# Rounding and an epsilon add given to GpSimd, and a different order of the first batch's parts, T4, weights and moved low parts, in a two-layer float32 kernel on one core

## The chip, the cores and the metric

The kernel runs on one core of one Trainium2 chip. The metric is device time in microseconds (us), from the first to the last instruction with what the launch adds around them; a smaller number is better. The engines are TensorE (PE), VectorE (DVE), ScalarE (ACT), GpSimd (POOL) and SyncE (SP), which only issues DMAs; ScalarE issues some DMAs too.

## The reference

There are 16 batches of 512 tokens with 512 features, in float32. Each batch names a language and an expert.

```python
# layer 0, per batch
h = relu(x @ aW1[lang] + ab1[lang])                  # 512 -> 128
u = x + h @ aW2[lang] + ab2[lang]                    # 128 -> 512
normed = (u - mean(u)) * rsqrt(var(u) + 1e-5)
x = x + normed * gamma[lang] + beta[lang]
# layer 1, per batch
h = gelu(x @ W1 + b1)                                # 512 -> 2048
out = x + concat(h @ W2 + b2, h @ We[expert] + be[expert])   # 2048 -> 384 and 128
```

## The kernel before

A float32 product is made of three passes in the type fp32r: every operand is split into a high part (HI, the value rounded) and a low part (LO, the value minus HI), and HI·HI, HI·LO and LO·HI are added up in PSUM (`three_passes`, L255 to L257). So every operand costs a rounding (an ACT copy, mostly) and a subtraction (DVE or POOL).

The batches go in eight pairs. For the second layer a pair is one matrix product by Strassen's scheme with seven products: x1 is cut into B11, B21, B22 and B12, their sums T1 to T4 take the place of some of them, and the weights W1 are kept with their sums S1 to S4. A pair has eight steps (k = 0 to 7, GROUPS = 8). Step k makes 4 x 128 of the hidden features: the products `pe_p1` to `pe_p7` into the banks up_a, up_b, up_c, and from them the tiles C11, C12, C22, C21. DVE adds the partial sums (`dve_sum_q`, `dve_sum_u2`, `dve_sum_c12`, `dve_sum_c22`, `dve_sum_c21`), ACT applies Gelu and rounds (`act_g`, `act_g_hi`), and DVE makes the low part (`dve_g_lo`, L899). `pe_down` then multiplies by W2 into the four `down` banks: C11 and C21 are the two halves (h = 0, 1) for the pair's batch 0, C12 and C22 for batch 1. `dve_down_sum` adds every second step's result to `resid`. Beside this, steps 0 to 7 do the first layer of the next pair (`pe_adapter_up`, `pe_adapter_down`, `dve_add_adapter`, `dve_moments`, `pool_rsqrt`, `dve_finish`).

The first pair is different. Its first layer runs ahead of everything else, and its W1 and W2 are rounded, summed and split while they are used: `pool_weight_sums(k)` makes S1 to S4 once the load has landed, `act_w1_hi(k)` rounds, `dve_w1_lo(k)` subtracts, `keep_w1` stores the result in DRAM for the later pairs, and `pe_p1` needs HI and then LO (`first_p1`, L299 and L307). For k = 1 and k = 8 (which is step 0 of the second pair) the subtraction is shared: `dve_rest_w1_lo` does four of the seven parts and `pool_first_w1_lo` the other three.

The first batch's bias b2 is added by a matmul: one row of b2 is rounded (`act_b2_hi`, L702), `dve_b2_lo` makes its low row (L957), and `pe_first_b2` (L505) multiplies by ones. In the first batch `act_first_part` copies each transposed block out of PSUM twice (L715 the value itself, L716 the rounded one), `pe_first_low` (L535) subtracts the rounded one in PSUM, and `act_first_low` (L720) copies the low part out. `first_hi` and `first_lo` (L276, L277, L282) are the products of step 0, collected by `first_half`.

The order of the work on each engine is written out by hand; each engine runs its list in order and waits on semaphores. An instruction that waits holds back all that stands behind it on its engine, DMA issues on ACT and SP included. `pool_rsqrt` waits for `dve_var`, the variance with epsilon added (L947, L976 on DVE), and takes it to the power of minus one half.

Of the kernel before, what the change touches and what calls it, by code (L numbers as in the profile page):

```python
# [26 lines left out]
def build(nc, xT, x, lang, expert, a_w1, a_b1, a_w2, a_b2, a_gamma, a_beta,  # L27
# [126 lines left out]
    dve_u, dve_st, dve_mv, dve_var, dve_gm, dve_x1 = (  # L154
        sem(n) for n in ("dve_u", "dve_st", "dve_mv", "dve_var", "dve_gm", "dve_x1"))
# [89 lines left out]
    FIRST_B11, FIRST_B21 = (up_a, down[1]), (down[2], down[1])  # L245
# [162 lines left out]
    def pe_down(eng, pr, b, k):  # L408
# [9 lines left out]
        for h in range(2):  # L418
# [19 lines left out]
        if opens:  # L438
# [500 lines left out]
    def dve_moments(eng, m, b, t):  # L939
# [7 lines left out]
        eng.tensor_scalar(var_eps[:, n - 1:n], mean_var[:, b, t, 1:2], EPS, None, ALU.add).then_inc(dve_var, 1)  # L947
# [20 lines left out]
    def dve_first_moments(eng, b, t, bank):  # L968
# [899 lines left out]
```

## Time and profile before

| | before |
|---|---|
| median of 3 runs | 1453.47 us (1453.41 to 1453.83) |
| the profiled execution | 1455.1 us |
| its span | 1453.3 us |
| PE busy | 1442.8 us, 99% |
| DVE busy | 949.9 us, 65% |
| POOL busy | 652.7 us, 45% |
| ACT busy | 524.8 us, 36% |
| granted TensorE clock | 1.0 in the whole span |

The profiled execution is the one that all rows come from. Its time is its span and 1.8 us around it. A row of a timeline gives the start in us from the span's start, the time in us, the engine, the line, the operation, output<-inputs and how many instructions it merges; in brackets stands the idle time of the engine before it, with what ended it.

### The profile page before, as it was taken

How to read it: one execution, taken by the hardware profiler on the slowest of the kernel's cores; microseconds unless marked ns; L12 is line 12 of the kernel's file. 1: busy time of each engine (PE TensorE's matmuls, PEld its weight loads, DVE VectorE, ACT ScalarE, POOL GpSimd, SP SyncE). 2: the span in 40 equal slices, each digit the busy share in tenths (PEclk: the TensorE clock that was granted, in tenths of full speed). 3: DMA queues.
4: the chain of work that ended last, by engine and by line, in shares of the span. 5: the costliest groups of instructions: out<-in, count | busy, mean ns of one | idle time of the engine just before them, and what ended most of it. 6: DMA issues, size and time to landing. Idle time of an engine off the chain costs nothing.

```text
span 1453.3 us, 19122 instructions
## 1 busy us (share of the span) xinstructions
PE 1442.8 (99%) x6444; PEld 1185.0 (82%) x6444; DVE 949.9 (65%) x1596; ACT 524.8 (36%) x854; POOL 652.7 (45%) x640
## 2 busy tenths in 40 slices
PE   9999999999999999999999999999999999999999
PEld 5778888888888888888888888888888888888887
DVE  6899786775567756667557675577656676554444
ACT  4633454232433225232352333433234322432231
POOL 5996466441473514834138341384323743341101
PEclk9999999999999999999999999999999999999999
DMA  7857577553466545564455644646446454364332
GB/s 237 272 165 243 180 245 249 171 195 132 167 224 182 185 148 178 202 212 148 159 192 186 206 151 154 231 146 213 177 137 236 156 191 159 109 218 159 131 109 87
DMA packets 127764, 263.02 MB, mean 181 GB/s; under 512 B 12210, under 2 KB 84402, under 8 KB 119604
## 3 DMA queue, kind: packets, MB, share of 16 engines
q1 hardware_dynamic: 117876, 158.78, 34.3%
q10 hardware_dynamic: 9792, 103.03, 18.3%
q8 instruction: 52, 0.85, 0.2%
q14 instruction: 44, 0.36, 0.1%
HBM read 224.02 MB, written 37.75 MB: 180 GB/s over the span
## 4 chain that ended last, share of the span: by engine, by line
PE 90%; DVE 3%; POOL 3%; issue 2%; ACT 1%; ACTq 0%; DMA 0%; SPq 0%; DVEq 0%; POOLq 0%
PE down L255 15%; PE down L257 15%; PE down L256 15%; PE up_b L255 5%; PE up_b L257 5%; PE up_b L256 5%; PE up_c L257 3%; PE up_c L256 3%; PE up_c L255 3%; PE up_a L255 3%; PE up_a L256 3%; PE up_a L257 3%; DVE g L899 1%; POOL resid L1270 1%; PE aux L518 1%
## 5 line engine op out<-in xcount | busy, mean ns | idle before, releaser
L255 PE MATMUL down<-w,g 128*128 128x512 f32 x1024 | 401.1, 392 | 0.9 <-DVE g L899 0.9
L257 PE MATMUL down<-w,g 128*128 128x512 f32 x1024 | 398.6, 389 | 0.0
L256 PE MATMUL down<-w,g 128*128 128x512 f32 x1024 | 398.5, 389 | 0.0
L1277 POOL TENSOR_TENSOR w<-w_raw,ones 128x256 fp32r<-128x256 f32 x128 | 90.5, 707 | 616.2 <-DMA w_raw<-m_we 616.1
L255 PEld LDWEIGHTS down<-w,g 128*128 128x128 f32 x1024 | 192.3, 188 | 42.4 <-DVE g L899 3.2
L899 DVE TENSOR_TENSOR g<-g_raw,g 128x512 fp32r<-128x512 f32 x256 | 211.4, 842 | 23.1 <-ACT g L671 20.9
L257 PEld LDWEIGHTS down<-w,g 128*128 128x128 f32 x1024 | 192.2, 188 | 40.3
L256 PEld LDWEIGHTS down<-w,g 128*128 128x128 f32 x1024 | 192.3, 188 | 39.0
L663 ACT ACTIVATE g_raw<-up_a,m_b_sb 128x512 f32<-128x512 f32 x64 | 44.1, 690 | 407.7 <-PE up_a L257 383.0
L894 DVE TENSOR_TENSOR g_raw<-up_b,s 128x512 f32<-128x512 f32 x63 | 43.5, 691 | 222.0 <-PE up_b L257 178.3
L671 ACT CAST g<-g_raw 128x512 fp32r<-128x512 f32 x256 | 159.0, 621 | 8.1
L663 ACT ACTIVATE g_raw<-u,m_b_sb 128x512 f32<-128x512 f32 x63 | 45.6, 724 | 252.0 <-PE down L257 230.6
L255 PE MATMUL up_b<-bo,w 128*128 128x512 f32 x336 | 131.6, 392 | 2.2 <-DVE u L879 1.4
L256 PE MATMUL up_b<-bo,w 128*128 128x512 f32 x336 | 130.8, 389 | 0.0
L257 PE MATMUL up_b<-bo,w 128*128 128x512 f32 x336 | 130.8, 389 | 0.0
L918 DVE TENSOR_TENSOR resid<-down,resid 128x512 f32<-128x512 f32 x128 | 86.6, 690 | 57.9 <-PE down L257 57.9
L1279 POOL TENSOR_TENSOR w<-w_raw,w 128x256 fp32r<-128x256 f32 x128 | 106.5, 832 | 10.1
L663 ACT ACTIVATE g_raw<-g_raw,m_b_sb 128x512 f32<-128x512 f32 x63 | 45.5, 722 | 161.0 <-DVE g_raw L894 161.0
L1270 POOL TENSOR_TENSOR resid<-x,m_bias 128x512 f32<-128x512 f32 x64 | 93.0, 1482 | 0.0
L257 PE MATMUL up_c<-bo,w 128*128 128x512 f32 x224 | 87.2, 389 | 0.0
L255 PE MATMUL up_c<-bo,w 128*128 128x512 f32 x224 | 87.2, 389 | 0.0
L256 PE MATMUL up_c<-bo,w 128*128 128x512 f32 x224 | 87.1, 389 | 0.0
(239 smaller groups left out, 2508.3 us busy)
## 6 DMA issues: line engine op xcount, KB each, us to landing
w<-w_kept ACTq DMA_DIRECT2D x55, 1792.0 KB, 7.6
w<-w_kept SPq DMA_DIRECT2D x56, 768.0 KB, 4.9
w_raw<-m_we SPq DMA_DIRECT2D x128, 128.0 KB, 4.6
out<-resid SPq DMA_DIRECT2D x64, 256.0 KB, 5.2
xTs_raw<-xT SPq DMA_DIRECT2D x56, 256.0 KB, 3.8
xs<-x SPq DMA_DIRECT2D x56, 256.0 KB, 4.9
w_kept<-w SPq DMA_DIRECT2D x8, 1792.0 KB, 7.7
aw_raw<-a_w SPq DMA_DIRECT2D x30, 256.0 KB, 4.5
```

Source lines behind the costliest of these rows:

```text
L255: eng.matmul(bank, a_hi, b_hi, start=opens, stop=False, skip_group_check=True)
L256: eng.matmul(bank, a_hi, b_lo, start=False, stop=False, skip_group_check=True)
L257: return eng.matmul(bank, a_lo, b_hi, start=False, stop=closes, skip_group_check=True)
L518: last = eng.transpose(bank[:, t * P:(t + 1) * P], x1[:, b, t, c * P:(c + 1) * P], ident[:, :])
L663: eng.activation(values, source, ACT.Gelu, bias=m_b1_sb[:, j:j + 1]).then_inc(act_gelu, 1)
L671: eng.copy(g[:, b, k % 2, h, HI, :], values).then_inc(act_ghi[b], 1)
L894: eng.tensor_tensor(g_raw[:, 0, k % 2, 1, LO, :], up_b[:, :], s1[:, :], ALU.add).then_inc(dve_c21, 1)
L899: eng.tensor_tensor(g[:, b, k % 2, h, LO, :], g_raw[:, b, k % 2, h, LO, :], raw(g[:, b, k % 2, h, HI, :]), ALU.subtract).then_inc(dve_glo[ ...
L918: eng.tensor_tensor(resid[:, 1, t, :], down[t][:, :], resid[:, 1, t, :], ALU.add).then_inc(dve_out[1], 1)
L1270: eng.tensor_tensor(resid[:, b, t, :], x1[:, b, t, :], m_bias[:, b, :], ALU.add).then_inc(pool_res, 1)
L1277: eng.tensor_tensor(hi, values, ones[:, :, :].to_broadcast([P, 2, PART]), ALU.mult).then_inc(pool_eh[b], 1)
L1279: eng.tensor_tensor(w2[:, k % 2, :, LO, cols], values, raw(hi), ALU.subtract).then_inc(pool_e[b], 1)
```

## The change

1. b2 is rounded by a GpSimd multiplication by ones (`pool_b2_hi`), not by an ACT copy. On ACT, `act_relu` of the first batch now stands ahead of the load of the second batch's aw.
2. The epsilon is added to each variance by GpSimd, inside `pool_rsqrt`; the DVE instruction is gone. GpSimd waits for itself between the add and the power.
3. In the first batch the rounded copies of B11 come before the kept ones, B11's second bank is waited for in a different place, and TensorE does six products with high parts earlier. C11's A11 part uses `down[3]` for the first block of B11.
4. The low part of W1 for k = 1 is made by DVE alone. T3's rounding moves ahead of the second step on ACT, and T3's low part ahead of aw's on GpSimd.
5. In the second step T4's rounding comes before that of xT, W1's before that of C12, and GpSimd's `pool_expert(1, 0)` after T4's low part.
6. The low parts of C12 and C22 of a step are made later on DVE: after `dve_sum_u2` where k is 1 to 3, ahead of the down sums where k is over 3. C21's comes first.
7. In the last pair's last step `pe_p4` stands between the two halves of `pe_down`.

```diff
@@ first_p1
-        if k == 1:
-            eng.wait_ge(pool_w1, 3)
-        else:
-            eng.wait_ge(dve_w1, k)
+        eng.wait_ge(dve_w1, k)
@@ pe_step
+        elif i is last_pair and k == GROUPS - 1:
+
+            pe_down(eng, i, 0, k - 1, (0,))
+            pe_p4(eng, i, k)
+            pe_down(eng, i, 0, k - 1, (1,))
+            return
@@ act_second_step
         act_first_sum(eng, i, 1)
-        act_aw_hi(eng, m, 0, 0)
-        for c in range(2):
-            act_t_hi(eng, i, T3, c)
         ...
         act_g(eng, i, 1, C11)
+        act_t_hi(eng, i, T4, 0)
+        act_t_hi(eng, i, T4, 1)
         act_xT_hi(eng, m, 0, 2)
         act_xT_hi(eng, m, 0, 3)
+        act_w1_hi(eng, 2)
+        act_g(eng, i, 1, C12)
         act_aw_hi(eng, m, 0, 1)
-        act_t_hi(eng, i, T4, 0)
-        act_t_hi(eng, i, T4, 1)
-        act_g(eng, i, 1, C12)
-        act_w1_hi(eng, 2)
         act_g(eng, i, 1, C22)
@@ dve_moments, and the same in dve_first_moments
-        eng.tensor_scalar(var_eps[:, n - 1:n], mean_var[:, b, t, 1:2], EPS, None, ALU.add).then_inc(dve_var, 1)
@@ dve_second_step
         dve_g_lo(eng, i, 1, C21)
-        dve_g_lo(eng, i, 0, C22)
@@ dve_first_step
-        if k > 2:
+        if k > 3:
             dve_g_lo(eng, i, k - 1, C12)
             dve_g_lo(eng, i, k - 1, C22)
         if k < GROUPS - 1:
             dve_sum_u2(eng, i, k)
-        else:
+        if k == 2:
+            dve_g_lo(eng, i, 0, C22)
+        if k == 3:
+            dve_g_lo(eng, i, k - 1, C12)
+            dve_g_lo(eng, i, k - 1, C22)
+        if k == GROUPS - 1:
@@ dve_step
             dve_sum_c21(eng, i, k - 1)
-            dve_g_lo(eng, i, k - 1, C12)
-            dve_g_lo(eng, i, k - 1, C22)
             dve_g_lo(eng, i, k - 1, C21)
         ...
+        if k > 3:
+            dve_g_lo(eng, i, k - 1, C12)
+            dve_g_lo(eng, i, k - 1, C22)
         if k % 2 == 0:
             if k >= 2:
                 dve_down_sum(eng, i, 0, k - 1)
         ...
         dve_sum_u2(eng, i, k)
+        if k in (1, 2, 3):
+            dve_g_lo(eng, i, k - 1, C12)
+            dve_g_lo(eng, i, k - 1, C22)
         dve_finishes(eng, m, k)
@@ new on GpSimd
+    def pool_b2_hi(eng):
+
+        eng.wait_ge(in_b2[0], 32)
+        eng.tensor_tensor(b2_row[:, HI, :], b2_row_raw[:, LO, :], ones[0:B2_ROWS, 0, :].to_broadcast([B2_ROWS, TOK]),
+                          ALU.mult).then_inc(pool_b2hi, 1)
@@ pool_rsqrt
-        eng.wait_ge(dve_var, m.count(2 * TT, n))
+        eng.wait_ge(dve_mv, m.count(2 * TT, n))
+        eng.tensor_scalar(var_eps[:, n - 1:n], mean_var[:, b, t, 1:2], EPS, None, ALU.add).then_inc(pool_var, 1)
+        eng.wait_ge(pool_var, m.count(2 * TT, n))
@@ pool_first_step
-            pool_first_w1_lo(eng, 2)
-            pool_aw_lo(eng, m, 0, 0)
             pool_t_lo(eng, i, T3, 0)
             pool_t_lo(eng, i, T3, 1)
+            pool_aw_lo(eng, m, 0, 0)
             pool_expert(eng, i, 0, 1)
-            pool_expert(eng, i, 1, 0)
             return
         if k == 1:
             pool_weight_sums(eng, 2)
             pool_t_lo(eng, i, T4, 0)
             pool_t_lo(eng, i, T4, 1)
+            pool_expert(eng, i, 1, 0)
@@ the first batch on TensorE
+            eng.wait_ge(pool_w1, 2)
+            for c in range(2):
+                eng.wait_ge(act_bhi, b_count(first, B11, c))
+                first_hi(eng, C11, A11, B11, c, c == 0)
             for c in range(2):
                 pe_first_low(eng, B11, c, FIRST_B11[c])
+            eng.wait_ge(act_bhi, b_count(first, B21, 0))
+            first_hi(eng, C11, A12, B21, 0, False)
             pe_first_low(eng, B21, 0, FIRST_B21[0])
-            pe_first_b12(eng, 0)
             eng.wait_ge(b_low, 2)
             pe_first_transpose(eng, B21, 1, FIRST_B21[1])
-            eng.wait_ge(pool_w1, 2)
-            first_half(eng, C11, A11, B11, True, False)
-            pe_first_low(eng, B21, 1, FIRST_B21[1])
+            for c in range(2):
+                first_lo(eng, C11, A11, B11, c, False)
+            pe_first_b12(eng, 0)
             pe_first_b12(eng, 1)
             first_half(eng, C21, A21, B11, True, False)
+            pe_first_low(eng, B21, 1, FIRST_B21[1])
@@ the first batch on ScalarE
-            act_first_part(eng, B11, 0, FIRST_B11[0])
-            act_first_part(eng, B11, 1, FIRST_B11[1])
-            act_first_part(eng, B21, 0, FIRST_B21[0])
+            for c in range(2):
+                act_first_hi(eng, B11, c, FIRST_B11[c])
+            for c in range(2):
+                act_first_keep(eng, B11, c, FIRST_B11[c])
+            act_first_hi(eng, B21, 0, FIRST_B21[0])
+            act_first_keep(eng, B21, 0, FIRST_B21[0])
@@ ahead of the steps on ScalarE
+            for c in range(2):
+                act_t_hi(eng, first, T3, c)
+            act_aw_hi(eng, pairs[1], 0, 0)
@@ ahead of the steps on VectorE
-            dve_rest_w1_lo(eng, 1)
+            dve_w1_lo(eng, 1)
```

## Rows read from the trace of the kernel before

**Rows 1.** The page, part 1: busy time, share, instructions.
```profile
PE 1442.8 (99%) x6444; PEld 1185.0 (82%) x6444; DVE 949.9 (65%) x1596; ACT 524.8 (36%) x854; POOL 652.7 (45%) x640
```

**Rows 2.** PE's waits: line waited for: us in total, times, longest.
```profile
PE up_b L255 <- DVE u L879: 1.4, 7, 0.3
PE down L255 <- DVE g L899: 0.9, 3, 0.5
PE up_b L255 <- POOL bo L1283: 0.8, 1, 0.8
PE down L505 <- issue: 0.6, 1, 0.6
PE up_a L307 <- DVE w L1067: 0.5, 1, 0.5
PE up_a L307 <- POOL w L1257: 0.5, 1, 0.5
```

**Rows 3.** PE's timeline from 0 to 70 us.
```profile
12.67 1.13 PE L513 MATMUL down<-aw_raw,h_raw 128*128 128x512 f32 x2
...
29.22 0.66 PE L525 MATMUL down<-ident,x 128*128 128x128 f32 x4 [0.20 <-ACT bo L720]
...
37.12 0.39 PE L276 MATMUL down<-bo,w 128*128 128x512 f32 x1
...
44.10 0.74 PE L307 MATMUL up_a<-bo,w 128*128 128x512 f32 x2 [0.48 <-POOL w L1257]
...
59.46 0.39 PE L257 MATMUL aux<-xTs,aw 128*128 128x512 f32 x1
60.66 0.47 PE L255 MATMUL up_b<-bo,w 128*128 128x512 f32 x1 [0.81 <-POOL bo L1283]
```

**Rows 4.** ACT's timeline, from 0 to 85 us.
```profile
10.14 0.62 ACT L702 CAST bo<-bo_raw 64x512 fp32r<-64x512 f32 x1 [5.83 <-issue]
...
11.34 0.69 ACT L688 ACTIVATE h_raw<-aux,a_b_sb 128x512 f32<-128x512 f32 x1 [0.59 <-PE aux L473]
...
81.22 1.70 ACT L772 CAST w<-w_raw 128x1792 fp32r<-128x1792 f32 x1 [5.27 <-POOL w_raw L1298]
```

**Rows 5.** POOL's timeline, from 0 to 85 us.
```profile
15.02 0.56 POOL L1263 TENSOR_TENSOR rstd<-var_eps,minus_half 128x1 f32<-128x1 f32 x1 [12.29 <-DVE var_eps L976]
...
23.10 1.27 POOL L1247 TENSOR_TENSOR x<-x,resid 128x512 f32<-128x512 f32 x1
...
57.68 2.84 POOL L1283 TENSOR_TENSOR bo<-bo_raw,bo 128x512 fp32r<-128x512 f32 x2
```

**Rows 6.** DVE's timeline, from 0 to 110 us.
```profile
14.79 0.15 DVE L976 TENSOR_SCALAR var_eps<-mean_var 128x1 f32<-128x1 f32 x1
14.86 0.75 DVE L979 SCALAR_TENSOR_TENSOR down<-down,mean_var,vecs 128x512 f32<-128x512 f32 x1
...
40.50 1.86 DVE L1039 TENSOR_TENSOR w<-w_raw,w 128x1024 fp32r<-128x1024 f32 x1 [0.22 <-ACT w L772]
...
83.46 3.11 DVE L1067 TENSOR_TENSOR w<-w_raw,w 128x1792 fp32r<-128x1792 f32 x1
...
98.35 1.28 DVE L899 TENSOR_TENSOR g<-g_raw,g 128x512 fp32r<-128x512 f32 x2
...
108.22 2.01 DVE L1067 TENSOR_TENSOR w<-w_raw,w 128x1792 fp32r<-128x1792 f32 x1
```

**Rows 7.** The windows from 90 to 100 us: PE, PEld, DVE, ACT, POOL busy.
```profile
90.00:100.00 10.00, 10.00 (x45) 8.03 (x43) 10.00 (x9) 3.98 (x7) 10.00 (x8) 1.00 1.01 353
```

**Rows 8.** PE's timeline in the second pair, steps 1 and 2.
```profile
248.95 0.50 PE L255 MATMUL down<-w,g 128*128 128x512 f32 x1 [0.49 <-DVE g L899]
...
259.81 0.39 PE L255 MATMUL up_c<-aw,h 128*128 128x512 f32 x1
```

**Rows 9.** DVE's timeline in the same stretch.
```profile
243.66 5.23 DVE L899 TENSOR_TENSOR g<-g_raw,g 128x512 fp32r<-128x512 f32 x3
...
256.29 0.69 DVE L884 TENSOR_TENSOR u<-up_c,u 128x512 f32<-128x512 f32 x1
```

More of the change, by code:

```diff
@@ L153, in build @@
     dve_xlo, dve_h0lo, b_low, dve_t = (sem(n) for n in ("dve_xlo", "dve_h0lo", "b_low", "dve_t"))
-    dve_u, dve_st, dve_mv, dve_var, dve_gm, dve_x1 = (
-        sem(n) for n in ("dve_u", "dve_st", "dve_mv", "dve_var", "dve_gm", "dve_x1"))
+    dve_u, dve_st, dve_mv, dve_gm, dve_x1 = (sem(n) for n in ("dve_u", "dve_st", "dve_mv", "dve_gm", "dve_x1"))
+    pool_var = sem("pool_var")
     dve_out = sems("dve_out", 2)
@@ L243, in build @@
     FIRST_BANKS = down, (up_b, up_c, aux, down[0])
-    FIRST_B11, FIRST_B21 = (up_a, down[1]), (down[2], down[1])
+    FIRST_B11, FIRST_B21 = (down[3], down[1]), (down[2], down[1])
     FIRST_B12, FIRST_B22 = (down[3], up_b), (aux, down[0])
@@ L338, in pe_p1 @@
         if i is pairs[1] and k == 0:
-            eng.wait_ge(pool_w1, 4)
+            eng.wait_ge(pool_w1, 3)
             eng.wait_ge(dve_w1, GROUPS)
@@ L406, in pe_p4, with pe_down @@
         up_product(eng, i, up_b, k, A22, T4, False, True).then_inc(pe_p[4], 1)
-    def pe_down(eng, pr, b, k):
+    def pe_down(eng, pr, b, k, halves=range(2)):
         opens, closes = k % 2 == 0, k % 2 == 1
@@ L417, in pe_down @@
         cols = slice(b * PART, b * PART + D)
-        for h in range(2):
+        for h in halves:
             eng.wait_ge(dve_glo[b], pr.count(2 * GROUPS, 2 * k + h + 1))
@@ L437, in pe_down @@
                     last.then_inc(pe_y[b], 1)
-        if opens:
+        if opens and 1 in halves:
             last.then_inc(pe_h[b], 1)
@@ L1034, in dve_first_t4, with dve_rest_w1_lo @@
         eng.tensor_tensor(bo_raw[:, T4, c, LO, :], b21_raw(c), t2_raw(c), ALU.subtract).then_inc(dve_t, 1)
-    def dve_rest_w1_lo(eng, k):
-        eng.wait_ge(act_w1hi, k)
-        eng.tensor_tensor(w1[:, k % 2, LO, A22:7, :], w1_raw[:, k % 2, LO, A22:7, :], raw(w1[:, k % 2, HI, A22:7, :]),
+    def dve_rest_w1_lo(eng):
+        eng.wait_ge(act_w1hi, GROUPS)
+        eng.tensor_tensor(w1[:, 0, LO, A22:7, :], w1_raw[:, 0, LO, A22:7, :], raw(w1[:, 0, HI, A22:7, :]),
                           ALU.subtract).then_inc(dve_w1, 1)
@@ L1141, in dve_first_step @@
             return
-        dve_rest_w1_lo(eng, GROUPS)
+        dve_rest_w1_lo(eng)
         dve_w2_lo(eng, k)
@@ L1251, in pool_first_w1_lo @@
         if n < 2:
-            slot, s = 0, slice(n * A22, n * A22 + 2)
+            s = slice(n * A22, n * A22 + 2)
             eng.wait_ge(act_first_w, n + 1)
         else:
-            slot, s = 3 - n, slice(A11, A22)
-            eng.wait_ge(act_w1hi, 1 if n == 2 else GROUPS)
-        eng.tensor_tensor(w1[:, slot, LO, s, :], w1_raw[:, slot, LO, s, :], raw(w1[:, slot, HI, s, :]),
+            s = slice(A11, A22)
+            eng.wait_ge(act_w1hi, GROUPS)
+        eng.tensor_tensor(w1[:, 0, LO, s, :], w1_raw[:, 0, LO, s, :], raw(w1[:, 0, HI, s, :]),
                           ALU.subtract).then_inc(pool_w1, 1)
@@ L1489, in keep_w1 @@
         eng.wait_ge(dve_w1, k)
-        if k in (1, GROUPS):
-            eng.wait_ge(pool_w1, 3 if k == 1 else 4)
+        if k == GROUPS:
+            eng.wait_ge(pool_w1, 3)
         eng.dma_start(raw(w1_kept[k % GROUPS, :, :, :, :]), raw(w1[:, k % 2, :, :, :])).then_inc(kept_w1[k % 2], 16)
@@ L1701, in _ @@
                 pe_transpose(eng, first, 1, 2 + c, FIRST_B22[c])
+            first_hi(eng, C11, A12, B21, 1, False)
             eng.wait_ge(b_low, 4)
-            first_half(eng, C11, A12, B21, False, True)
+            for c in range(2):
+                first_lo(eng, C11, A12, B21, c, c == 1)
             first_half(eng, C21, A22, B21, False, True)
@@ L1719, in _ @@
             load_b2_column(eng, language)
-            act_b2_hi(eng)
             load_b1(eng, first, 1, language)
+            act_relu(eng, first, 0)
             load_aw(eng, first, 1, 1, language)
-            act_relu(eng, first, 0)
             load_first_beta(eng, 1, language)
@@ L1739, in _ @@
             act_w2_hi(eng, 1)
-            act_first_part(eng, B21, 1, FIRST_B21[1])
+            act_first_hi(eng, B21, 1, FIRST_B21[1])
+            act_first_keep(eng, B21, 1, FIRST_B21[1])
             for c in range(2):
@@ L1757, in _ @@
                 act_xT_hi(eng, pairs[1], 0, c)
+            for c in range(2):
+                act_t_hi(eng, first, T3, c)
+            act_aw_hi(eng, pairs[1], 0, 0)
             run(eng, act_step)
@@ L1810, in _ @@
                               base=0, pattern=[[-1, P]], channel_multiplier=1).then_inc(pool_minus, 1)
+            pool_b2_hi(eng)
             pool_rsqrt(eng, first, 0, 0)
```

16 lines of the change are left out of this document (6 added, 10 removed).

## The prediction

> **What bounds the kernel now.** I read the page first: TensorE is busy 1442.8 of 1453.3 us in 6444 matmuls, no other engine over 65% [rows 1]. No product is added or taken away, so the time can only fall by what TensorE loses between its instructions. The second view is TensorE's waits: some 5 us in about 15 waits, most on VectorE and GpSimd [rows 2]. The third is TensorE's timeline, for what a wait really costs: the matmul at 59.46 should be followed 0.23 us later (1442.8 us in 6444 steps [rows 1]), at 59.69, and the next starts at 60.66, so the wait listed with 0.81 us costs 0.97 [rows 3]. I add 0.16 us to every listed wait. All waits together then are some 7.8 us; this is the most that the change can win, 0.54%.
>
> Last come the other engines' timelines around each wait. In the first pair VectorE and GpSimd are both full: 10.00 of 10 us each from 90 to 100 us [rows 7]. There a stall that is removed hands the limit to them. In later pairs they have room.
>
> **The change, part by part.**
>
> *b2 (the 0.6 us wait).* ScalarE could round b2 only at 10.14, after issuing its own DMAs ("issue" ended its idle time) [rows 4]; VectorE's low row and TensorE follow. GpSimd is idle then. The trace does not show its new instruction; the nearest row is 1.27 us for 128x512 [rows 5], and I take that. When b2 lands no row says, but by 10.14 at the latest. If earlier than about 9, b2 is no limit and the next one is Relu: it starts when TensorE's product is done, 11.34, and ends at 12.03 [rows 4], so the first `L513` matmul starts near 12.10, not at 12.67 [rows 3]: 0.57 us. If b2 lands at 10.14, the chain is 10.14 + 1.27 + 0.69 for VectorE (as at 256.29 [rows 9]) + two matmuls, about 13.0: 0.3 lost. I take 0.57, since nothing but the issues shows as holding ScalarE. The aw load that moves behind Relu is issued 0.6 us later; nothing waited for it.
>
> *Epsilon.* VectorE loses an instruction of 0.15 us, but the next starts 0.07 us later (14.79, 14.86), so 0.07 us comes free, 64 times [rows 6]. GpSimd gains one plus a wait for itself. Its price lies between 0.10 us (nearly free) and the 0.56 us of its power on the same shape [rows 5]; I take 0.2. In the first batches GpSimd runs without a pause from about 21 to 30 us, and five such adds make its last root 1 us later there (0.5 to 2.8), less the 0.5 us by which it starts earlier: VectorE's last finish comes 0.5 us late, ahead of the need for it.
> [...] No row here shows this add on GpSimd.
>
> *The first batch.* The transposes at 29.22 wait for ScalarE's low copies [rows 3]. ScalarE's chain starts from a load, not from b2, so they stay at about 29.2, and the 0.57 us is lost there. But six matmuls of 0.23 us (1.36) now stand ahead and only two transposes (0.22) move behind: the group at 37.12 starts about 1.15 us earlier. Bounds: 0.5 (ScalarE's copies later) to 1.4.
>
> *W1 for k = 1 (0.5 us).* TensorE waits at 44.10 for GpSimd's three parts [rows 3]. VectorE now does all seven: a whole W1 took it 2.01 us beside an idle GpSimd and 3.11 beside a busy one [rows 6]. It starts near 40.0 (40.50 less ScalarE's 0.5) and ends between 42.0 and 43.1; TensorE wants it at 44.10 - 0.64 - 1.15 = 42.3. I take 0.45 of the 0.64. Behind it VectorE's xT low parts and q come up to 1 us later; q is wanted 3 us after. Lead at 44 us: 1.6 us.
>
> *T4 (0.8 us) and W1 for k = 2 (0.5 us).* GpSimd's T4 low part ran at 57.68 behind two experts and the sums [rows 5]. With 2.8 us of W1 work and one expert gone from ahead of it, the sums start when their load lands, about 51, and T4 is done at about 57; TensorE wants it at 58.1. ScalarE rounds W1 right after, so VectorE's 3.1 us end about a microsecond ahead of need. Both waits go: 0.97 + 0.69. Lead 3.3 us.
>
> *The rest of the first pair.* Waits for g, u and u again are worth 0.4 + 0.7 and would make the lead 4.4. Here the limit is handed on. GpSimd's expert (1, 0), 1.9 us, now stands behind T4, so of its 3.3 us only about 1.3 arrive at the sums for k = 3, and ScalarE's rounding at 81.22 [rows 4] moves to 79.9; VectorE's W1 at 83.46 moves by 1.9 and its chain from there to 100 us has no pause. The moved low parts (1.28 us at 98.35 [rows 6]) let u come 3.2 us earlier in all; then the down sums and c12, which the adapter's second product waits for, are 0.5 us late again. Lead at the end of the pair: 2.7 us, bounds 1.5 (adds at 0.56 us, GpSimd's chain no faster) and 4.4 (nothing handed on).
>
> *The later pairs.* In step 2 VectorE made three low parts in 5.23 us, C21's last [rows 9], and TensorE waited 0.49 us for it [rows 8]. C21's now comes first: it must wait for ScalarE (about 1.5 us), then 1.74, so it is ready 1.9 us earlier, and everything up to u too. Five waits for u (0.2 + 0.16 each), one for g (0.65) and two hidden delays of 0.15 make 2.8 us in seven pairs.
>
> *The last step* (one of the three waits on g): `pe_p4` 2.7 us earlier lets C21's Gelu and low part run under 12 matmuls: 0.36 us.
>
> *Sum:* 2.7 + 2.8 + 0.36 = 5.9 us; I keep 0.4 us back, since VectorE's two moved parts collide in some pair. Against the profiled execution (1455.1 us, span 1453.3) this is 1449.6; the runs' median lies 1.6 us lower, so I forecast 1453.5 - 5.5 = 1448.0 us.
>
> **The rivals.**
>
> *All stalls go:* 7.8 us less, 1445.7. For it: VectorE idles some 3 us before W1 for k = 2, a store of time. Against it: both engines are full from 90 to 100 us [rows 7].
>
> *GpSimd holds the first pair:* its adds at 0.56 us and its experts beside a busy VectorE keep the sums for k = 3 where they are. Then the lead at 80 us falls back to about 1, the later pairs' 2.8 stay: 1453.5 - 1 - 2.8 = 1449.7, up to 1451 if some waits for u stay too.
>
> *Not what it says:* the waits for g and u of the later pairs have other causes (their phase against GpSimd's residual work), and move instead of going. Then 2.7 less 1 in the first pair is all: 1451.8.
>
> *Slower:* the two low parts now stand between u and c12 in steps 1 to 3, 2 x 1.74 = 3.5 us beside a busy GpSimd. c12 ended at 256.98 [rows 9] and the adapter's product that needs it started at 259.81 [rows 8]: 2.8 us of slack. If C21's part is not earlier by the 1.9 us, c12 is 0.7 us late plus what TensorE has gained; at 1.0 to 1.5 us in seven pairs that is 7 to 10 us lost, less 2.7: 1458 to 1461. It decides from 2.8 us of added work on; with the 1.9 us it adds 1.6. For it: such long low parts are there; against it: most were 0.7 us where GpSimd was idle.
>
> **How the numbers follow.** Forecast, 5.5 us less, itself 1446.5 to 1449.5: 0.55. All stalls gone: 0.08. GpSimd holds: 0.17. Not what it says, or a 0 to 2.9 us gain in another way: 0.14. Slower: 0.06. A measurement of this kernel can tell 0.2% (2.9 us, 1450.6) from no change. Faster takes the first two and nearly all of the third: 0.78; same 0.16; slower 0.06. The range goes from 1445.8 to 1451.5, and leaves out the slow case and half of "not what it says".
>
> **What would show it.** In the trace of the changed kernel: the `L513` matmul near 12.1; the group of 37.12 near 36; no wait on L307; T4's product without a wait near 58; no wait for g at the second pair's step 2 and none in the last step; u's waits gone in the later pairs. A new wait for W1 at k = 3 near 84 us, or for u or c12 near 96 to 101 us, would show the limit handed on. The prediction is wrong if waits on c12 stand in every pair, if GpSimd's add takes over 0.5 us, or if b2 lands near 10 us.

## The result, and the profile after

The changed kernel takes 1465.13 us (median; 1462.83 to 1468.98) against 1453.44 us for the kernel before, a ratio of 1.0084 [1.0066, 1.0103]. The forecast was 1448.0. It is slower, and on the wrong side.

The profiled execution took 1462.83 us with a span of 1461.0 us, 7.7 more than before. The first line is the page's part 1; under it stand TensorE's waits.

```profile
PE 1443.1 (99%) x6444; PEld 1186.3 (81%) x6444; DVE 965.8 (66%) x1532; ACT 523.3 (36%) x853; POOL 688.2 (47%) x704
```
```profile
PE aux L255 <- DVE xTs L921: 7.9, 8, 1.7
PE aux L255 <- POOL aw L1232: 2.9, 2, 2.3
...
PE down L255 <- DVE w L1067: 1.0, 2, 0.7
PE up_a L255 <- issue: 0.5, 1, 0.5
PE down L521 <- ACT bo L720: 0.2, 1, 0.2
PE up_a L304 <- DVE w L1062: 0.2, 1, 0.2
```

TensorE's work is what it was [rows 1]; only its gaps changed. The waits of before for u, for g, for T4 and for W1 of k = 2 are gone [rows 2]. In their place stand two for the adapter weight's low part and, above all, eight for `xTs`, the low parts of the next pair's transposed x, which no row of before names.

**Where the time went.** I take the start of step 0 of each pair from TensorE's timeline (its first product; the last column is from there to the end of the span). An undisturbed pair is 177.74 us.

| us | first pair ends | the six later pairs | rest | span |
|---|---|---|---|---|
| before | 198.23 | 179.11, 177.75, 178.55, 178.23, 178.56, 178.37 | 184.5 | 1453.3 |
| after | 198.77 | 177.74, 182.35, 177.74, 180.13, 180.49, 179.82 | 184.0 | 1461.0 |

Two of the six are now free of stalls, and the rest is 0.5 us shorter. Four are 2.1 to 4.6 us too long: 11.8 us together, where before lost 4.1 us in all six. The sum is +0.5 + 11.8 - 4.1 - 0.5 = +7.7 us, the whole difference of the spans.

**What stands in the long pairs.** TensorE's timeline in the second of the six, step 1; then VectorE and GpSimd in the same stretch:

```profile
412.67 0.39 PE L257 MATMUL up_b<-bo,w 128*128 128x512 f32 x1
414.78 0.50 PE L255 MATMUL aux<-xTs,aw 128*128 128x512 f32 x1 [1.72 <-DVE xTs L921]
...
416.46 0.79 PE L255 MATMUL aux<-xTs,aw 128*128 128x512 f32 x1 [0.72 <-DVE xTs L921]
...
417.91 0.63 PE L255 MATMUL down<-w,g 128*128 128x512 f32 x1
418.33 0.63 PE L256 MATMUL down<-w,g 128*128 128x512 f32 x1
```
```profile
409.02 0.69 DVE L876 TENSOR_TENSOR u<-up_b,s 128x512 f32<-128x512 f32 x1 [0.67 <-PE up_b L257]
409.62 3.43 DVE L896 TENSOR_TENSOR g<-g_raw,g 128x512 fp32r<-128x512 f32 x2
412.98 3.43 DVE L921 TENSOR_TENSOR xTs<-xTs_raw,xTs 128x512 fp32r<-128x512 f32 x2
```
```profile
408.27 5.90 POOL L1281 TENSOR_TENSOR resid<-x,m_bias 128x512 f32<-128x512 f32 x4
```

VectorE finishes u and then, by the new order, makes the low parts of C12 and C22 (L896) before the two of xT (L921). Beside them GpSimd adds the residual of the pair's first batch (to 414.17) and makes the low part of an adapter weight (to 415.86), and each subtraction takes 1.7 us. The `aux` products could come at 412.9, right behind `up_b`; their xT low parts are done near 414.7 and 416.4. In the trace of before VectorE went straight from u to xT at this point; VectorE, then TensorE:

```profile
410.45 3.18 DVE L924 TENSOR_TENSOR xTs<-xTs_raw,xTs 128x512 fp32r<-128x512 f32 x2
```
```profile
413.72 0.39 PE L255 MATMUL aux<-xTs,aw 128*128 128x512 f32 x1
...
414.40 0.39 PE L255 MATMUL aux<-xTs,aw 128*128 128x512 f32 x1
```

The second xT low part ended at 413.63 there and was needed at 414.40: 0.8 us of slack, in one pair of one execution. The change puts 3.4 us in front of it.

One of the long pairs is far longer than its waits. The windows right behind the first wait show why (PE, PEld, DVE, ACT, POOL busy, then the granted clock, DMA share, GB/s):

```profile
412.00:417.00 5.00, 2.56 (x9) 1.54 (x8) 5.00 (x5) 0.00 (x0) 4.92 (x5) 0.95 0.86 305
417.00:419.00 2.00, 2.00 (x6) 1.55 (x5) 1.24 (x3) 1.93 (x3) 2.00 (x2) 0.50 0.19 70
```

TensorE was busy 2.56 of 5 us, and then its granted clock was 0.50, the 1.2 GHz level, until about 420: matmuls 0.43 us apart instead of 0.227. The two waits cost 1.88 and 0.89 us (listed with 1.72 and 0.72), 2.77 of this pair's 4.61; 1.7 of the other 1.84 are the slow matmuls. In the other three long pairs the clock stayed up, and the two waits of each (they cost 2.2, 2.5 and 1.8 us) are all but 0.3 of the loss.

The third of the six pairs has no wait at all. VectorE, then GpSimd:

```profile
591.96 1.28 DVE L896 TENSOR_TENSOR g<-g_raw,g 128x512 fp32r<-128x512 f32 x2
593.16 2.25 DVE L921 TENSOR_TENSOR xTs<-xTs_raw,xTs 128x512 fp32r<-128x512 f32 x2
```
```profile
592.57 1.15 POOL L1288 TENSOR_TENSOR w<-w_raw,ones 128x256 fp32r<-128x256 f32 x1 [2.46 <-DMA w_raw<-m_we]
...
594.82 3.55 POOL L1281 TENSOR_TENSOR resid<-x,m_bias 128x512 f32<-128x512 f32 x2
```

GpSimd waited 2.46 us for an expert weight, so its residual adds began 3.5 us after u (u at 591.35), where they began 0.7 us ahead of it in the pair above (408.27 and 409.02). L896's two low parts then took 0.64 us each and L921's two 1.1. In this execution the same order was harmless in one pair and cost 4.6 us in another, by when a DMA landed.

### The profile page after: what moved, and what is told of

It is laid out like the page before. It is cut to its first block, busy times and chain, and to the rows that moved or that the text cites. A ratio compares the mean times of both kernels' runs of the same rounds, so it can differ in the third digit from the quotient of the medians.

```text
span 1461.0 us, 19138 instructions
## 1 busy us (share of the span) xinstructions
PE 1443.1 (99%) x6444; PEld 1186.3 (81%) x6444; DVE 965.8 (66%) x1532; ACT 523.3 (36%) x853; POOL 688.2 (47%) x704
## 4 chain that ended last, share of the span: by engine, by line
PE 88%; POOL 6%; DVE 3%; issue 2%; ACT 1%; DMA 0%; SPq 0%; POOLq 0%; DVEq 0%; ACTq 0%
PE down L255 15%; PE down L257 15%; PE down L256 15%; PE up_b L257 5%; PE up_b L255 5%; PE up_b L256 5%; PE up_c L257 3%; PE up_c L255 3%; PE up_c L256 3%; PE up_a L257 3%; PE up_a L255 3%; PE up_a L256 3%; POOL resid L1281 1%; PE aux L514 1%; POOL xs L1243 1%
## 5 line engine op out<-in xcount | busy, mean ns | idle before, releaser
L1288 POOL TENSOR_TENSOR w<-w_raw,ones 128x256 fp32r<-128x256 f32 x128 | 94.9, 741 | 586.6 <-DMA w_raw<-m_we 586.6
L896 DVE TENSOR_TENSOR g<-g_raw,g 128x512 fp32r<-128x512 f32 x256 | 233.8, 934 | 85.7 <-ACT g L673 85.7
L915 DVE TENSOR_TENSOR resid<-down,resid 128x512 f32<-128x512 f32 x128 | 85.0, 687 | 35.7 <-PE down L257 35.7
```

Of the source, the lines that this page charges most:

```text
L896: eng.tensor_tensor(g[:, b, k % 2, h, LO, :], g_raw[:, b, k % 2, h, LO, :], raw(g[:, b, k % 2, h, HI, :]), ALU.subtract).then_inc(dve_glo[ ...
L915: eng.tensor_tensor(resid[:, 1, t, :], down[t][:, :], resid[:, 1, t, :], ALU.add).then_inc(dve_out[1], 1)
L1288: eng.tensor_tensor(hi, values, ones[:, :, :].to_broadcast([P, 2, PART]), ALU.mult).then_inc(pool_eh[b], 1)
```

## The experiments

The theory after the result was A (its name in the expectations): the loss is the low parts of C12 and C22 ahead of those of xT in step 1, made long by the residual adds beside them. The rivals were the epsilon adds on GpSimd (B, later E), a clock that falls by itself (C), a loss that needs the other moves too (D), and the wait at 76.5 us in the first pair with the clock behind it (G). Each table row is a kernel; the columns are those of the table above, and the medians and ratios are against the kernel before on the same chip.

| kernel | median us | ratio | first pair ends | six later pairs, sum | span |
|---|---|---|---|---|---|
| e1_xt_first | 1452.54 | 0.9994 [0.9984, 1.0004] | 199.0 | 1066.5 | 1449.4 |
| e2_before_k1_only | 1463.73 | 1.0066 [1.0045, 1.0088] | 198.1 | 1079.9 | 1462.5 |
| e3_eps_on_vector | 1462.15 | 1.0056 [1.0040, 1.0071] | 201.0 | 1070.7 | 1455.6 |
| e5_short_residual | 1453.31 | 0.9994 [0.9983, 1.0004] | 202.0 | 1067.1 | 1453.0 |
| e6_before_eps_pool | 1455.49 | 1.0013 [1.0003, 1.0022] | 199.6 | 1067.9 | 1451.9 |
| e7_aw_earlier | 1452.20 | 0.9987 [0.9978, 0.9996] | 200.2 | 1068.7 | 1452.8 |
| e8_gpsimd_order | 1452.83 | 0.9992 [0.9983, 1.0001] | 198.9 | 1066.5 | 1449.4 |
| e9_vector_order_old | 1457.59 | 1.0026 [1.0016, 1.0035] | 200.7 | 1071.0 | 1455.7 |
| e10_old_order_aw_earlier | 1458.79 | 1.0027 [1.0014, 1.0041] | 199.2 | 1071.0 | 1454.1 |
| e11_later_pairs_only | 1451.33 | 0.9984 [0.9975, 0.9993] | 199.5 | 1067.5 | 1450.9 |
| e12_all_mended | 1451.14 | 0.9989 [0.9980, 0.9998] | 197.2 | 1067.4 | 1448.6 |
| after_again | 1459.36 | 1.0032 [1.0021, 1.0043] | 201.2 | 1071.5 | 1456.7 |
| e13_old_order_eps_back | 1454.73 | 0.9997 [0.9988, 1.0007] | 198.1 | 1069.9 | 1452.0 |

Before has 198.2, 1070.6 and 1453.3. The first pair of e11 has the instructions of before and ends 1.2 us later than before's; the first pair of after_again ends 2.5 us later than that of the same kernel's first profile. A difference of a microsecond in that column proves nothing by itself.

### The cause in the later pairs

**e1_xt_first.** The changed kernel with two calls moved.

```diff
         dve_sum_u2(eng, i, k)
+        if m and k == 1:
+            dve_xT_lo(eng, m, 0, 2)
+            dve_xT_lo(eng, m, 0, 3)
         if k in (1, 2, 3):
             dve_g_lo(eng, i, k - 1, C12)
             dve_g_lo(eng, i, k - 1, C22)
         dve_finishes(eng, m, k)
-        if m and k == 1:
-            dve_xT_lo(eng, m, 0, 2)
-            dve_xT_lo(eng, m, 0, 3)
```

> The changed kernel with one edit: in step 1 of the later pairs VectorE makes the two xT low parts right after u, and the two moved low parts of C12 and C22 behind them. Theory A (the two moved low parts, slow beside GpSimd's residual adds, hold back the xT low parts that the adapter's products wait for in step 1): the waits of aux on xTs near 414, 774, 954 and 1134 us go, all of pairs 1 to 6 take 177.7 us, the span falls from 1461.0 by some 11.8 us to about 1449.2, the granted clock is 1.0, and the runs agree within 0.5 us, near 1451. Rival B (GpSimd's epsilon adds are what costs): no change, 1463 to 1469. Rival C (the clock falls by itself and the waits are a by-product): some runs still 2 to 6 us above the others, with a clock under 1.0.

Measured: 1452.54 us, 0.9994 [0.9984, 1.0004], 12.6 us less than the changed kernel's first set of runs and 6.8 less than its second (after_again, below). The profiled span was 1449.4. All six later pairs took 177.74 to 177.77 us, and no wait for `xTs` is left among TensorE's waits:

```profile
PE aux L255 <- POOL aw L1232: 3.0, 2, 2.4
...
PE down L255 <- DVE w L1067: 0.9, 2, 0.7
```

VectorE's timeline shows the long low parts still there, but in the other order, ending ahead of the need for c12, which is the row of L881:

```profile
409.86 2.46 DVE L921 TENSOR_TENSOR xTs<-xTs_raw,xTs 128x512 fp32r<-128x512 f32 x2
412.25 3.47 DVE L896 TENSOR_TENSOR g<-g_raw,g 128x512 fp32r<-128x512 f32 x2
415.64 0.68 DVE L881 TENSOR_TENSOR u<-up_c,u 128x512 f32<-128x512 f32 x1
```

So the order of four instructions is the loss. With these four in the other order the change as a whole has no effect on the median that can be told from none: against before, the later pairs of this profile gain 4.1 us and the first pair loses 0.8.

**e2_before_k1_only.** The kernel before with this move alone.

```diff
             dve_sum_c21(eng, i, k - 1)
-            dve_g_lo(eng, i, k - 1, C12)
-            dve_g_lo(eng, i, k - 1, C22)
+            if k > 1:
+                dve_g_lo(eng, i, k - 1, C12)
+                dve_g_lo(eng, i, k - 1, C22)
...
         dve_sum_u2(eng, i, k)
+        if k == 1:
+            dve_g_lo(eng, i, 0, C12)
+            dve_g_lo(eng, i, 0, C22)
```

> The kernel before with one part of the change alone: in step 1 of the later pairs the low parts of C12 and C22 are made behind u, ahead of xT's; steps 2 and on as before. Theory A: the adapter's products in step 1 wait for xT in three to five of the six pairs, 1 to 3 us each, and the time is 1457 to 1468, with a clock under 1.0 in some runs. Rival B (epsilon adds) and rival D (it needs the other moves together): 1453 to 1454.

Measured: 1463.73 us, 1.0066 [1.0045, 1.0088]; the six later pairs took 9.4 us longer than before's. TensorE's waits begin with the same line:

```profile
PE aux L255 <- DVE xTs L924: 7.6, 9, 1.4
```

The move alone, in a kernel that has nothing else of the change, makes a loss of the same size: the intervals of the two ratios overlap.

**e5_short_residual.** The changed kernel; GpSimd's residual adds of the first batch of every later pair cover 32 of 512 columns, and the rest of that sum is left out.

```diff
-        eng.tensor_tensor(resid[:, b, t, :], x1[:, b, t, :], m_bias[:, b, :], ALU.add).then_inc(pool_res, 1)
+        w = 32 if b == 0 and i is not first else D
+        eng.tensor_tensor(resid[:, b, t, 0:w], x1[:, b, t, 0:w], m_bias[:, b, 0:w], ALU.add).then_inc(pool_res, 1)
```

> The changed kernel, in which GpSimd adds the residual of each later pair's first batch in 32 of 512 columns only (the other columns of that sum are left out of the output). VectorE's order is as in the changed kernel. If sharing with GpSimd is what makes the two moved low parts long (1.7 us each and not 0.65), they take 1.3 us together, the waits for xT in step 1 go, and the span is near 1449 to 1451. If the order alone does it, the waits stay near 1 to 2 us and the span near 1458 to 1461.

Measured: 1453.31 us, 0.9994 [0.9983, 1.0004]. No wait for `xTs`; five of the six later pairs took 177.74 us. With the order of the changed kernel untouched, VectorE's xT low parts are short again:

```profile
415.76 1.28 DVE L921 TENSOR_TENSOR xTs<-xTs_raw,xTs 128x512 fp32r<-128x512 f32 x2
```

In the same place the two moved low parts in front of it took 2.38 us, beside the low part of an adapter weight on GpSimd. Order and GpSimd's long adds are both needed: without the adds the four low parts take at most 3.7 us and all fit; with them they took 6.8 from 409.62 in the changed kernel. The edit also brings GpSimd's later work forward, so it doesn't separate contention in the adds from contention in what follows them. The median hides that the first pair of this execution ended at 202.0, behind a wait of 4.1 us.

### Epsilon and the first pair

**e3_eps_on_vector.** The changed kernel with the epsilon add back on VectorE.

> The changed kernel with epsilon added on VectorE again, all else as changed. Theory A: the later pairs keep their waits for xT, only the first pair gains: its waits near 113, 125 and 158 us (0.9, 0.65, 0.4 us with what follows) go or shrink, so 1 to 2 us less than the changed kernel, 1461 to 1467. Rival B: the time falls to 1455 or under.

Measured: 1462.15 us, 1.0056 [1.0040, 1.0071], far from before; its ten runs spread from 1455.37 to 1465.79. The profiled execution has these waits:

```profile
PE aux L255 <- POOL aw L1234: 4.7, 2, 4.1
...
PE aux L255 <- DVE xTs L921: 1.9, 4, 0.5
```

The xT waits are there, smaller than in the changed kernel. Its profiled span, of one of the shortest runs, was 5.4 us under the changed kernel's, its median 3 us. The median lies 7 us above what rival B asks for (1455 or under), so the epsilon adds aren't the main loss; since the size of the xT waits varies by itself (after_again, below), this doesn't size epsilon.

**e6_before_eps_pool.** The kernel before with the epsilon add moved to GpSimd, as in the change, and nothing else.

```diff
-        eng.tensor_scalar(var_eps[:, n - 1:n], mean_var[:, b, t, 1:2], EPS, None, ALU.add).then_inc(dve_var, 1)
...
     def pool_rsqrt(eng, m, b, t):
         n = b * TT + t + 1
+        eng.wait_ge(dve_mv, m.count(2 * TT, n))
+        eng.tensor_scalar(var_eps[:, n - 1:n], mean_var[:, b, t, 1:2], EPS, None, ALU.add).then_inc(dve_var, 1)
         eng.wait_ge(dve_var, m.count(2 * TT, n))
```

> The kernel before with the epsilon add alone moved to GpSimd. Theory E (in the first pair GpSimd's chain sets the pace, and each add costs 0.2 us there when VectorE is quiet and up to 0.8 us beside it): waits appear in the first pair from 113 us on and the first pair ends 0.5 to 1.5 us later; the later pairs are as before. Time 1454 to 1455.5, so 0 to 0.1% above before. Rival (VectorE's 0.07 us per tile decide): 1452 to 1453.5.

Measured: 1455.49 us, 1.0013 [1.0003, 1.0022]: epsilon on GpSimd costs 0.4 to 3.2 us by itself. It is a loss, but a small one, and the profile doesn't show where: it is of the shortest of the ten runs, with the first pair 1.3 us later than before's and the six later pairs 2.7 us shorter.

**e7_aw_earlier.** e1 with the low part of the adapter weight (1, 0) ahead of the bias adds on GpSimd, which takes away the wait of 2.29 us at 76.52.

```diff
+            pool_aw_lo(eng, m, 1, 0)
             pool_biases(eng, m, 0, 0)
             pool_biases(eng, m, 0, 1)
-            pool_aw_lo(eng, m, 1, 0)
```

> The changed kernel with VectorE's xT low parts first in step 1 (as in e1_xt_first), and GpSimd's low part of the adapter weight (1, 0) ahead of the two pairs of bias adds in the first pair's second step. Theory F (GpSimd's chain to W1 for k = 4 is the limit, the 2.4 us wait near 76.7 us only shows it early): that wait goes, the waits near 113 and 125 us grow by about the same 2 us, and the first pair ends at 198.7 to 199.2 us as in e1_xt_first; time within 1 us of it. Rival G (the wait near 76.7 us is a loss of its own): the first pair ends at 196.5 us, the time is 2.4 us less.

Measured: 1452.20 us, 0.9987 [0.9978, 0.9996], not to be told from e1. The wait is gone, and others took its place:

```profile
PE up_c L255 <- DVE u L881: 2.0, 2, 1.5
PE up_a L304 <- DVE w L1062: 1.8, 2, 1.5
```

**e8_gpsimd_order.** e7, and on GpSimd the weight sums for k = 4 ahead of the roots in step 3, and aw (0, 0) between T3's two low parts.

```diff
+        if k == 3:
+            pool_weight_sums(eng, 4)
         pool_roots(eng, m, k)
```

> As e7_aw_earlier, and in the first pair GpSimd makes the weight sums for k = 4 ahead of the roots and experts of step 3, and the adapter weight's low part between T3's two. Theory F: W1 for k = 4 is rounded some 4 us earlier, the waits near 48, 77 and 113 us go, the one near 125 us shrinks, the first pair ends between 196 and 198 us, and the time is 1 to 3 us below e1_xt_first, 1449.5 to 1451.5. Rival H (VectorE's own full list holds the first pair): no gain over e1_xt_first.

Measured: 1452.83 us, 0.9992 [0.9983, 1.0001]; span and first pair (198.9) as in e1. The waits for W1 (1.8 us) and for u stayed. The likely reason is that VectorE has no pause in this stretch [rows 7], so that work fed to it earlier is not done earlier; that is argued, not shown.

**e12_all_mended.** e8 with the epsilon add back on VectorE, and in steps 1 to 3 one moved low part on each side of `dve_sum_c12`.

```diff
         if k in (1, 2, 3):
             dve_g_lo(eng, i, k - 1, C12)
-            dve_g_lo(eng, i, k - 1, C22)
         dve_finishes(eng, m, k)
         dve_sum_c12(eng, i, k)
+        if k in (1, 2, 3):
+            dve_g_lo(eng, i, k - 1, C22)
```

> The changed kernel with all that the runs found mended: xT low parts first in step 1, one moved low part on either side of the sum of c12, epsilon on VectorE, and GpSimd's order of e8_gpsimd_order in the first pair. Theory: the first pair ends near 197 to 198 us, later pairs at 177.74, clock 1.0: 1448.5 to 1451. If the first pair's gain can't be had (VectorE full), it equals e7_aw_earlier, 1452.

Measured: 1451.14 us, 0.9989 [0.9980, 0.9998], and the shortest profiled span, 1448.6 us, with the earliest end of the first pair, 197.2.

**e11_later_pairs_only.** The kernel before with only the new order in the later pairs, xT's low parts first in step 1, and the split last step.

> The kernel before with only two parts: VectorE's low parts of C12 and C22 later in the later pairs (in step 1 behind the xT low parts), and the fourth product between the halves of the last step. Nothing changed in the first pair. Theory A: pairs 1 to 6 take 177.74 us each (before 177.75 to 179.11), the last step's wait of 0.2 us goes: 3.5 to 4.5 us less than before, near 1450. Rival (the gain of the later pairs needs the changed first pair): 1453 to 1454.

Measured: 1451.33 us, 0.9984 [0.9975, 0.9993]. Its six later pairs took 1067.5 us (177.89 to 177.93 each, where 177.74 was expected), 3.1 less than before's, and the rest 0.5 less. Its first pair, with before's instructions, ended 1.2 us later: TensorE waited 1.84 us for T4's low part there (0.81 in before), and the granted clock was 0.50 from 63.1 to 66.5. This part alone wins all that any of these kernels wins, 1.0 to 3.6 us. e11, e7 and e12 beat both kernels; their intervals don't tell them apart.

### The size of the loss, and a miss

**after_again.** The changed kernel in another set of runs, on another chip than e1 to e9. On which chip the first set ran is not on record.

> The changed kernel itself, on the same chip and beside the same runs of before as the experiments of this call. Theory A: 1462 to 1469 again, and in the profiled execution the adapter's products of step 1 wait for xT in at least three of the six pairs, in places that need not be the ones seen before (they depend on whether GpSimd's residual adds fall beside VectorE's moved low parts); a step whose residual adds come late shows none.

Measured: 1459.36 us, 1.0032 [1.0021, 1.0043]. The sign holds; the size is less than half. TensorE's waits:

```profile
PE aux L255 <- POOL aw L1232: 4.7, 2, 4.1
PE aux L255 <- DVE xTs L921: 2.8, 6, 0.7
```

The xT waits are short here, and GpSimd's timeline shows why: in the fourth of the six pairs it waited 2.42 us for an expert weight and began the residual adds at 772.11, 2.9 us after u (769.24); in the first profile of this kernel it began them at 768.93, 0.2 us ahead of u (769.09). The fifth pair differs in the same way. Over the two profiles of this kernel, pairs lost 2.1 to 4.6 us where the residual adds began ahead of u, 0.8 to 1.5 where they began 1.8 to 2.9 us behind it, and nothing where they began 3.5 us or more behind it. The wait for the adapter weight is longer, and the clock fell behind it (windows from 74 us on):

```profile
74.00:78.60 4.60, 0.55 (x3) 0.12 (x1) 2.26 (x4) 0.00 (x0) 4.52 (x5) 0.92 0.00 0
78.60:82.00 3.40, 3.35 (x8) 2.68 (x9) 0.00 (x0) 0.51 (x1) 3.32 (x5) 0.50 0.00 0
82.00:84.00 2.00, 2.00 (x7) 1.52 (x6) 0.69 (x1) 1.18 (x1) 1.92 (x3) 0.50 0.62 222
```

**e9_vector_order_old.** The changed kernel with VectorE's old order in the later pairs; all else of the change stays.

```diff
             dve_sum_c21(eng, i, k - 1)
+            dve_g_lo(eng, i, k - 1, C12)
+            dve_g_lo(eng, i, k - 1, C22)
             dve_g_lo(eng, i, k - 1, C21)
...
-        if k > 3:
-            dve_g_lo(eng, i, k - 1, C12)
-            dve_g_lo(eng, i, k - 1, C22)
...
-        if k in (1, 2, 3):
-            dve_g_lo(eng, i, k - 1, C12)
-            dve_g_lo(eng, i, k - 1, C22)
```

> The changed kernel with VectorE's order in the later pairs as before (low parts of C12 and C22 right after the sum of C21), all else changed. Theory A: no waits for xT; the waits for g and u of the kernel before are back in step 2 (0.35 to 1.0 us a pair, 3.5 us in all), the first pair ends near 198.8, the last step keeps its 0.4 us gain: 1452.5 to 1454.5. Rival (the changes of the first pair cost the most): 1458 or more.

Measured: 1457.59 us, 1.0026 [1.0016, 1.0035]; a miss, 3 us over the expectation. The later pairs are as before, with the waits for u and g back. The first pair ended 2.5 us late, after a wait of 4.1 us for the adapter weight and slow matmuls behind it. That made G a theory for these 3 us. With the old order in the later pairs the kernel is still 0.26% slower than before, so the change has a second, smaller loss outside that order.

**e10_old_order_aw_earlier.** e9 with the adapter weight's low part moved as in e7.

> As e9_vector_order_old (the changed kernel with VectorE's old order in the later pairs, 1457.6), and GpSimd's low part of the adapter weight (1, 0) ahead of the bias adds. Theory G (the wait near 77 us, 2.3 to 4.1 us long, is what the first pair loses: the granted clock falls behind it): the wait goes, the clock is 1.0 in nearly all runs, and the time is 1453 to 1455.5. Theory F (GpSimd's chain behind it is the limit anyway): 1457 to 1458.

Measured: 1458.79 us, 1.0027 [1.0014, 1.0041]. The profile did what G wants: the long wait is gone, the first pair ends 1.6 us earlier, the clock stays up. The time didn't follow, so G isn't borne out. A second profiled execution, on another chip, was a short one too:

> The kernel of e10_old_order_aw_earlier again, for a profile of an execution near its median of 1458.8 us (its first profile was of a short one, 1455.9). Theory E: the later pairs show waits of TensorE on VectorE's finishes or sums behind GpSimd's roots. Rival: they show longer waits for g and u in step 2, up to 1.5 us a pair.

Measured: 1455.5 us, span 1453.7, first pair 199.9, the six later ones 1069.8. The longest wait of its later pairs is 0.26 us, so neither theory shows, but the execution isn't one near the median either.

**e13_old_order_eps_back.** e10 with the epsilon add back on VectorE.

> As e10_old_order_aw_earlier (1458.8 us: VectorE's old order in the later pairs, the first pair changed, the adapter weight's low part early), with epsilon on VectorE again. Theory E (the epsilon adds on GpSimd are what is left of the loss of about 4 us): 1453.5 to 1455. Rival (the old order and the changed first pair lose it without the adds): 1457 to 1459.

Measured: 1454.73 us, 0.9997 [0.9988, 1.0007]. Beside e10's 1.0027 this points to epsilon, as e6 does; but e10 and e13 ran on different chips, and the two intervals nearly touch. The one execution of e10 on e13's chip (e10_again, 1455.5) lies within e13's ten (1453.52 to 1456.45), so this pair of kernels doesn't show epsilon's share. e10's median lies 3 us over both of its profiled executions, so what makes it longer is in no profile here. Why e9 and e10 are slower than before stays open in part.

## Why the prediction was wrong, step by step

*The later pairs: the step that failed.* The forecast read step 2, where the removal frees C21, and stopped there. The move reaches into step 1 too, where the two low parts land ahead of xT's. The prediction's own price, 2 x 1.74 = 3.5 us beside a busy GpSimd, was right (3.43 measured), and it charged this, in its rival "slower", to c12, which has 2.8 us of slack. Nothing was charged to what stands on VectorE between u and c12. With the row of before at 410.45, the same price gives 3.5 less 0.8 of slack, 2.7 us in each pair where the residual adds fall there. The four long pairs lost 1.8 to 2.8 us in waits; e1 and e2 show that this step is the cause. The rival "slower" had mechanism and size, but the wrong victim, and so the point from which it decides was put at 2.8 us where it was 0.8. Its chance of 0.06 was too low by that.

*What it forecast of these pairs beyond that came true.* With xT first, the waits for u and g are gone and the six pairs take 1066.5 us, 4.1 less than before; in seven pairs 2.8 had been taken. The price of a wait was too low: the step behind it took 0.34 us and not 0.227 (248.95 to 249.29, and so behind each wait of these pairs), so a wait cost its listed time and 0.27 us, not 0.16. The last step's 0.36 was 0.5 for the same reason.

*b2 and the first batch.* `L513` is L509 in the changed kernel. TensorE's timeline:

```profile
11.93 1.12 PE L509 MATMUL down<-aw_raw,h_raw 128*128 128x512 f32 x2
...
35.92 0.39 PE L276 MATMUL down<-bo,w 128*128 128x512 f32 x1
...
42.65 0.73 PE L304 MATMUL up_a<-bo,w 128*128 128x512 f32 x2 [0.23 <-DVE w L1062]
```

11.93 against 12.10 forecast; the group of 37.12 came 1.20 earlier (1.15 forecast) [rows 3]; W1 for k = 1 is waited for 0.23 us, and the lead there was 1.45 (1.6 forecast). GpSimd's product of b2 started at 8.07 and took 1.03 us, so b2 was no limit. T4 and W1 for k = 2 have no wait. So far the sum held, but for one row:

```profile
48.08 0.50 PE L255 MATMUL aux<-xTs,aw 128*128 128x512 f32 x1 [0.59 <-POOL aw L1232]
```

T3's low part now stands ahead of this adapter weight's on GpSimd (part 4 of the change), and no term had the price of that: TensorE's lead fell from 1.45 us to 0.63. Behind W1 for k = 2, at 61.6 us, it was 2.4 where 3.3 had been forecast.

*The rest of the first pair: a lead of 2.7 us was forecast, and it ended 0.5 late.* GpSimd before, then after:

```profile
76.64 1.30 POOL L1229 TENSOR_TENSOR aw<-aw_raw,aw 128x512 fp32r<-128x512 f32 x1
...
97.84 1.59 POOL L1263 TENSOR_TENSOR rstd<-var_eps,minus_half 128x1 f32<-128x1 f32 x2
99.41 0.70 POOL L1277 TENSOR_TENSOR w<-w_raw,ones 128x256 fp32r<-128x256 f32 x1
```
```profile
75.20 1.26 POOL L1232 TENSOR_TENSOR aw<-aw_raw,aw 128x512 fp32r<-128x512 f32 x1
...
96.40 0.65 POOL L1272 TENSOR_SCALAR var_eps<-mean_var 128x1 f32<-128x1 f32 x1
97.13 0.57 POOL L1274 TENSOR_TENSOR rstd<-var_eps,minus_half 128x1 f32<-128x1 f32 x1
97.68 0.57 POOL L1272 TENSOR_SCALAR var_eps<-mean_var 128x1 f32<-128x1 f32 x1
98.34 0.86 POOL L1274 TENSOR_TENSOR rstd<-var_eps,minus_half 128x1 f32<-128x1 f32 x1
99.16 0.61 POOL L1288 TENSOR_TENSOR w<-w_raw,ones 128x256 fp32r<-128x256 f32 x1
```

GpSimd's chain moved by 1.44 us at the adapter weight; 1.3 had been forecast. What was overlooked is that TensorE needs this weight on the way: in before its low part ended at 77.94 and the product started at 78.00, a limit with hardly a wait to its name. TensorE would have been 3.9 us ahead there and was 1.5 us ahead (the wait of 2.29 us at 76.52). That is the mechanism of the rival "GpSimd holds the first pair", at another weight than it named.

The second term is epsilon. Ahead of the two roots GpSimd led by 1.44 us, behind them by 0.25: the two adds cost 1.2 us here, 0.6 each, three times the 0.2 that was taken and just over the upper bound of 0.56. Behind the adds the sums for k = 4 took 0.85 us longer than before (two of them 1.19 and 1.18 us at 102.65 and 103.80, against 0.73 and 0.74), which had no term either. Other VectorE work lies beside them than before; whether that is why is not shown. So ScalarE rounded this W1 at 106.16, 0.59 us later than before, and VectorE sat idle for it for 1.17 us.

TensorE's lead then went as follows: 1.5 us at 76.5; 1.95 at 98.7, where before had waited for u; 0.86 behind a wait for VectorE's W2 at 113.05; 0.1 behind the one at 124.72; 0.5 late behind another for VectorE's weights at 157.90. The middle one is listed under "issue" but ended with GpSimd's low part of a third adapter weight:

```profile
124.72 0.47 PE L255 MATMUL up_a<-aw,h 128*128 128x512 f32 x1 [0.50 <-issue]
```
```profile
123.33 1.29 POOL L1232 TENSOR_TENSOR aw<-aw_raw,aw 128x512 fp32r<-128x512 f32 x1
```

Epsilon is on this path too, but how much of the 2.4 us between 98.7 and 158 it owns is not shown: of the two kernels that only move it back, e13 ended the first pair 1.1 us earlier than e10, but e3's first pair has a wait of 4.1 us that the first profile doesn't have.

The price of the add has two levels. 43 of the 64 adds took 0.21 to 0.23 us, 24 of them beside the down sums (L915), which read a PSUM bank; 21 took 0.57 to 0.78, and each of these began beside a VectorE instruction with all its tensors in SBUF (L946, L896 or L921). VectorE's own add took 0.15 [rows 6]. The Trainium skill's "GPSIMD Engine Reference", section Engine selection, has elementwise work on VectorE, with GpSimd about twice as slow for operations with two inputs and roughly as fast for one. This add has one tensor input, and for so small an instruction the trace doesn't agree: it took 1.4 times as long as VectorE's at the least (0.21 us), and four to five times as long beside the instructions named. An add over 0.5 us was one of the forecast's own signs of being wrong.

*A cost that no term had.* The clock: TensorE ran at 1.0 through the whole profile of before, and the sum knew waits only at their length and 0.16 us. Behind such waits the changed kernel needed 3.52 us for eight steps of 0.227 (416.46 to 419.98), 1.7 us lost, and after_again 6.08 us for fourteen (78.65 to 84.73), 2.9 lost.

## What to carry to other kernels

When work is moved on an engine that runs its list in order, list every instruction that it is put in front of, in each step where the new order holds, with its consumer's start and its own end; the slack that decides is the smallest of them, and a limit can show no wait to warn of it (the adapter weight of 77.94, needed at 78.00). Price the moved work at its duration beside the other engine's load, not at its usual one. Here a saving of 0.1 to 0.2% (e7, e11, e12) stood against a loss of 0.3 to 0.8% by an order of four instructions, and the same four in another order took the loss away.

## What the runs showed of the hardware

- A VectorE subtraction of 128x512 in SBUF took 0.64 us beside an idle GpSimd and 1.7 us beside its adds (pairs of 1.28 and of 3.43 us).
- TensorE's granted clock fell from 1.0 to 0.50 (from the 2.4 to the 1.2 GHz level) behind waits of 1.72 and 0.72 us in one step (changed kernel, 416.5) and with a wait of 4.10 us (after_again); the slow matmuls went on for 3.5 and 6.1 us. Behind a wait of 2.29 us (changed kernel, 76.5), and behind waits of 1.45 and 0.73 us (954.7 and 956.4), it stayed at 1.0.
- An add of one element per partition on GpSimd took 0.22 us in the median and up to 0.78 (in the row: shortest, median and longest in ns); all 64 together took 24.7 us, 0.39 each:

```profile
L1272 POOL TENSOR_SCALAR var_eps<-mean_var x64: 212/222/782, 14.1 to 1232.0; 128x1 f32<-128x1 f32 x64
```

- The same kernel lost 0.84% in one set of runs and 0.32% in another. What varied in the traces was when the expert weights landed, and with it which GpSimd work lay beside VectorE's.
